# Blocks 0 and 1 of a masked graph kernel: first-layer result, e1 sums, table and first batches placed one slot sooner

## The chip, the cores and the metric

One NeuronCore of one Trainium2 chip runs the whole program. The metric is the device time in microseconds (us) of one execution; the median of three runs is compared.

## The reference, cut to what matters

`x` is 8192 by 128 in float32, `adj` 8192 by 8192 in int32, symmetric, with about 0.2% of entries 1 and the rest 0. Two graph layers follow each other, each with a residual and a normalization of the rows.

```python
o = (adj == 1) @ (x @ w1) + (adj == 2) @ (x @ w2) + (adj == 3) @ (x @ w3) + bias
x = layernorm(x + o)
h = x @ W.T + b
e = (h @ we1 + be1) + (h @ we2 + be2).T
e = where(e >= 0, e, 0.01 * e)
attention = softmax(where(adj > 0, e, -9e15), axis=1)
x = layernorm(x + attention @ h)
```

## The kernel before, in words

**Blocks, chunks and slots.** The 8192 rows are 8 blocks (S) of 1024, each block's columns 8 chunks of 1024. Every engine's program is written out by hand as one loop over slots `k`. In slots 0 to 63 slot k takes in chunk k: GpSimd (POOL) issues the load of 1 MB (`load`, L527 to L535; four homes, so load k waits until chunk k-4 is packed), VectorE (DVE) packs it into bits (`check_and_pack`, L586 to L617), ScalarE (ACT) converts it (`convert`, L1121), TensorE (PE) turns it (`turn`, L1348), and ACT copies it out of PSUM one slot later (`edges_of`, L1136). One slot later DVE makes the two halves of 0/1 masks of chunk k-1 (`edge_masks`, L630), and two slots later PE multiplies them in 32 matmuls, 16 a half (`layer0(k-2, h)`, L1333). `turn` is of blocks 0 to 3 alone; later blocks are turned by DMA.

**The tail of a block.** `tails(k)` (L360) gives for each slot the blocks S and their offset `off = k - 8(S+1)`. At off 1 ACT copies the block's sums (`y_of`, L1154) and PE multiplies them by w1 (`o_of(S, 0)`, L1355) into PSUM bank 3. At off 2 DVE adds x (`v_of(S, 0)`), PE makes `o_of(S, 1)` into the same bank between the two halves of layer0, having waited for `v_of(S, 0)`, and after packing DVE runs `v_of(S, 1)`, `statistics` (L670) and, at the slot's end, `rs_of` (L682), with ACT's square root `sd_of` (L1162) between them. At off 3 ACT writes the normalized rows x1 (`x1_of`, L1166), DVE forms the sums with two vectors (`e_sums`, L688: products at L693, sums at L697 and L700, constants at L704 and L707), between its two mask halves, and PE turns e1 (`e1_turn`, L1369) at the end of its slot. At off 4 ACT copies e1 out (`e1_turned`, L1182), makes exponentials (`b_d_of`) and the high half of the block's table (`high`, L1187); DVE makes the low half (`low`, L718) at off 4 in block 0 and off 5 in block 1; in later blocks its two parts come at off 5 and 6. SyncE (SP) stores x1 and then e1 (`tail`, L399), and reads e1 back as a row on all partitions (`row_of`, L416).

**Batches.** The second layer is 128 batches (`batch(m)`, L1374) of 32 matmuls, one group of 512 rows with one chunk of columns. A batch needs the table of its chunk, the group's e1 row, eight ACT passes over that row (`gates`, L1140), and four bit passes and two logical passes on DVE (`masks`, L639). 48 of them are spread over slots 13 to 68, the rest runs from slot 69 with one batch a slot. `EARLY` (L57) says which batches come behind which block, and `plan` (L72) puts block b's first one in slot `8(b+1) + START` with START 5. Batches 0 and 1 stand in slots 13 and 14; batches 2 to 7 in slots 21, 22, 23, 25, 26 and 27; from slot 29 every slot has one. Block b's first batch is `fresh` (L126): its gates come after `convert` on ACT, those of other batches before it, in the slot ahead. The very first batch is placed behind the turning (`first_of_all`, L131). The sums of batch segment q go to banks 4 and 5 for even q, 6 and 7 for odd q (`z_bank`, L249), and DVE takes them out a batch later (`collect`, L754). At the end of a slot in which a segment ends, DVE prepares its exponents (`exponents`, L732), for which the partial sum before must have been stored.

**Order on a queue.** Each engine takes its instructions strictly in the order written. What stands behind a waiting instruction waits too.

Of the kernel before, what the change touches and what calls it, by code (L numbers as in the profile page):

```python
# [31 lines left out]
NS = 8  # L32
# [22 lines left out]
START = 5  # L55

EARLY = {  # L57
# [14 lines left out]
def plan():  # L72

    segs, slots, seen = [], [], {}
    for b, part in EARLY.items():
        segs += part
        n = sum(len(c) for _, c in part)
        slots += [NCH * (b + 1) + START + (i * NCH // n if n >= 6 else i) for i in range(n)]
        for g, c in part:
            seen.setdefault(g, set()).update(c)  # L80
    for g in LATE:
        segs.append((g, [c for c in range(NS) if c not in seen.get(g, ())]))
    early = len(slots)
    slots += [max(K + START, slots[-1] + 1) + i for i in range(16 * NS - early)]
    return segs, slots
# [40 lines left out]
def fresh(m):  # L126

    return SLOTS[m] == NCH * (BATCH[m][1] // 2 + 1) + START

# [11 lines left out]
def build(nc, x, adj, w1, w2, w3, bias, W, b, we1, be1, we2, be2, out):  # L141
# [4 lines left out]
    with ExitStack() as ctx:  # L146
# [98 lines left out]
        def o_of_bank(S, h):  # L245

            return ps[:, 2, :].rearrange("p (t c) -> p t c", t=GT) if h and S >= PAIRS else o_bank

# [128 lines left out]
        def _(e):  # L377
# [20 lines left out]

            def tail(S):  # L399
                e.wait_ge(s_x1, S + 1)  # L400
                e.dma_start(block_rows(x1_dram, S), X1[:, :, :]).then_inc(s_x1st, 16)
                e.wait_ge(s_e1Tc, S + 1)
                e.dma_start(e1_dram[S], e1T[:, :]).then_inc(s_e1st, 16)

# [54 lines left out]
            for S in range(NS - 1):  # L459
                tail(S)  # L460
                row_of(q)
                next_rows(S)
                for n in range(len(EARLY[S])):
                    if n + 1 < len(EARLY[S]):
                        row_of(q + 1)
                    if q:
                        part_store(q - 1)
                    part_load(q)
                    q += 1
            for S in STAGED:  # L470
                table_load(S)
            row_of(LOWS)
            tail(NS - 1)
            row_of(LOWS + 1)
# [98 lines left out]
        def _(e):  # L573
# [114 lines left out]
            def e_sums(S, parts=(0, 1)):  # L688
                sl = slice(JC * S, JC * (S + 1))
                e.wait_ge(s_x1, S + 1)  # L690
                e.wait_ge(s_setc, 1)
                for n in parts:
                    e.tensor_tensor((yT8, xg[:, :, :])[n], X1[:, :, :],  # L693
                                    u_b[:, n, :].unsqueeze(1).broadcast_to([P, RB, D]), ALU.mult).then_inc(s_pe, 1)
                if 0 in parts:
                    e.wait_ge(s_pe, 2 * S + 1)
                    e.reduce_sum(e1c[:, sl], yT8, AX).then_inc(s_e1c, 1)  # L697
                if 1 in parts:
                    e.wait_ge(s_pe, 2 * S + 2)
                    e.reduce_sum(t2[:, sl], xg[:, :, :], AX).then_inc(s_er, 1)  # L700
                if 0 in parts:
                    e.wait_ge(s_setc, 2)
                    e.wait_ge(s_e1c, 2 * S + 1)
                    e.tensor_scalar(e1c[:, sl], e1c[:, sl], c_sum[:, :], None, ALU.add).then_inc(s_e1c, 1)  # L704
                if 1 in parts:
                    e.wait_ge(s_er, S + 1)
                    e.tensor_scalar(t2c[:, sl], t2[:, sl], T2MAX, -T2MAX, ALU.min, ALU.max).then_inc(s_t2c, 1)  # L707
# [228 lines left out]
            for k in range(NSLOT):  # L936
                for S, off in tails(k):
                    if off == 2 and S < NS - 1:
                        v_of(S, 0)
                for m in at(k):  # L940
                    if not first_of_all(m):
                        masks(m)
                        after(m)
# [4 lines left out]
                for S, off in tails(k):  # L948
                    if off == 2:
                        if S == NS - 1:  # L950
                            v_of(S, 0)
                        v_of(S, 1)
                if 1 <= k <= K:
                    edge_masks(k - 1, 0)
                for S, off in tails(k):
                    if off == 2:
                        statistics(S)
                    if off == 3 and S < NS - 1:
                        e_sums(S)
                    if off == 3 and S == NS - 1:  # L960
                        rs_of(S)
                    if off in (4, 6) and S == NS - 1:
                        e_sums(S, ((off - 4) // 2,))
# [10 lines left out]
                for S, off in tails(k):  # L974
                    if off == 0:
                        x_and_bias(S)
                    if off == 2 and S < NS - 1:
                        rs_of(S)
                    if (S, off) in ((0, 4), (1, 5)):
                        low(S)  # L980
# [129 lines left out]
        def _(e):  # L1110
# [136 lines left out]
            for k in range(NSLOT):  # L1247
                for S, off in tails(k):
                    if off == 3 and S < NS - 1:
                        x1_of(S)  # L1250
# [4 lines left out]
                for S, off in tails(k):  # L1255
                    if off == (4 if S < NS - 1 else 6):
                        e1_turned(S)
                    if off == (4 if S < NS - 1 else 7):
                        b_d_of(S)
# [3 lines left out]
                for S, off in tails(k):  # L1263
                    if off == 4 and not S:
                        high(S)
                if k < PAIRS * NCH:
                    convert(k)
                elif k < K:
                    turn_pairs(k)
                for S, off in tails(k):  # L1270
                    if off == 2:
                        sd_of(S)
                if k < NCH:
                    split_high(k)
                for S, off in tails(k):
                    if off == 1:
                        y_of(S)
                    if off == 4 and 0 < S < NS - 1:
                        high(S, (0,))
# [6 lines left out]
                for S, off in tails(k):  # L1286
                    if off == 4 and 0 < S < NS - 1:
                        high(S, (2,))
                    if off == 3 and S == NS - 1:
                        x1_of(S)  # L1290
# [41 lines left out]
        def _(e):  # L1332
# [22 lines left out]
            def o_of(S, h):  # L1355
                e.wait_ge(s_y, 2 * S + h + 1)
                if h:
                    if S < PAIRS:
                        e.wait_ge(s_v, 2 * S + 1)
# [14 lines left out]
            def batch(m):  # L1374
# [5 lines left out]
                if first:  # L1380
                    ge(e, s_ev, q - 1)
                    if q == 0:
                        e.wait_ge(s_setc, 1)
                e.wait_ge(s_pos, m + 1)
                both = UP[:, 4096 * (m % 2):4096 * (m % 2 + 1)], gate_bufs[GATE[m]]
# [54 lines left out]
            for k in range(NSLOT):  # L1440
                if 2 <= k < K + 2:
                    layer0(k - 2, 0)
                for S, off in tails(k):
                    if off == 4 and PAIRS <= S < NS - 1:
                        e1_turn(S)
                    if off == 2 and S < NS - 1:
                        o_of(S, 1)
# [12 lines left out]
                for S, off in tails(k):  # L1460
                    if off == 1:
                        o_of(S, 0)
                        if S == NS - 1:
                            o_of(S, 1)
                    if off == 3 and S < PAIRS or off == 5 and S == NS - 1:
                        e1_turn(S)
# [99 lines left out]
```

## Time and profile before

| | |
|---|---|
| three runs | 1488.92, 1488.93, 1489.4 us, median 1488.93 |
| profiled execution | 1488.94 us, of which 1487.3 us lie between first and last instruction |
| granted TensorE clock, mean | 0.987 |
| busy time | PE 1391.1 us, DVE 1120.1, ACT 922.0, POOL 64.3 |
| loads of adj | 64, of 1 MB each in the kernel's memory |

The share of a busy engine is an average over stages: one with loads and one slot after another, and one with batches alone. An idle stretch of PE counts only where nothing later absorbs it.

### The profile page before, as it was taken

What the parts mean: (1) busy time and instruction counts of PE and PEld (TensorE: products, weight loads), DVE (VectorE), ACT (ScalarE), POOL (GpSimd) and SP (SyncE); (2) the same over time, 40 slices, a digit from 0 to 9 for tenths busy, and PEclk for the clock granted to TensorE, in tenths of its full rate; (3) what the DMA queues carried; (4) which work ended last, traced back from release to release, by engine and by line L of the source; (5) the groups of instructions that cost most, each with busy time, mean ns of one, the idle gap of its engine ahead of it and who ended that gap; (6) DMA issues with size and microseconds to landing.
All of it is one profiled execution on the core that took longest, in us unless ns stands there. A gap on an engine that the chain in (4) does not pass through costs nothing.

```text
span 1487.3 us, 18911 instructions
## 1 busy us (share of the span) xinstructions
PE 1391.1 (94%) x6678; PEld 651.6 (44%) x6678; DVE 1120.1 (75%) x2568; ACT 922.0 (62%) x1521; POOL 64.3 (4%) x73
## 2 busy tenths in 40 slices
PE   0787898999999999999999999999999999999996
PEld 0333343444444444444444444444444444444443
DVE  2668777988988978978978957776666777776664
ACT  1333525466546436345345459887888989988873
POOL 1101010000000000000000000000000000000000
PEclk9999899999999999999999999999999999999998
DMA  9999999996989989997999521000000111110000
GB/s 124 148 117 117 117 112 127 120 121 83 92 112 118 95 88 110 103 126 84 116 112 111 99 99 43 22 29 29 29 29 29 50 29 36 50 29 22 22 0 16
DMA packets 104786, 115.86 MB, mean 78 GB/s; under 512 B 21424, under 2 KB 87792, under 8 KB 104688
## 3 DMA queue, kind: packets, MB, share of 16 engines
q0 software_dynamic: 66560, 67.11, 49.5%
q1 hardware_dynamic: 20720, 43.30, 8.7%
q10 hardware_dynamic: 17408, 4.20, 1.8%
q8 instruction: 55, 0.90, 0.2%
q14 instruction: 43, 0.35, 0.1%
HBM read 295.44 MB, written 16.29 MB: 210 GB/s over the span
## 4 chain that ended last, share of the span: by engine, by line
PE 78%; DMA 9%; DVE 7%; ACT 4%; issue 2%; another core or an unknown queue 0%; POOL 0%; ACTq 0%; DVEq 0%; SPq 0%; POOLq 0%
PE ps L1389 56%; PE ps L1342 20%; DMA tables<-adj 8%; ACT neg_masks L1149 2%; DVE edge_masks L627 1%; PE ps L1404 1%; DVE seen L594 1%; PE ps L1366 1%; DVE neg_masks L647 1%; DVE tables L725 1%; DVE tables L591 0%; ACT tables L1198 0%; DVE adj_in L591 0%; ACT x L1172 0%; PE ps L1352 0%
## 5 line engine op out<-in xcount | busy, mean ns | idle before, releaser
L1149 ACT ACTIVATE neg_masks<-e_row,cols 128x512 int8<-128x512 f32 x816 | 510.6, 709 | 183.7 <-PE ps L1389 134.3
L1389 PE MATMUL ps<-pos_masks,tables 128*128 128x512 fp8e4 x2048 | 610.4, 380 | 7.5 <-DVE pos_masks L649 7.4
L1389 PE MATMUL ps<-neg_masks,tables 128*128 128x512 fp8e4 x1632 | 486.5, 380 | 0.0
L1342 PE MATMUL ps<-edge_masks,tables 128*128 128x512 fp8e4 (+1 forms) x2048 | 463.3, 384 | 0.0
L1389 PEld LDWEIGHTS ps<-pos_masks,tables 128*128 128x128 f16 x2048 | 200.0, 98 | 247.8 <-issue 12.7
L1342 PEld LDWEIGHTS ps<-edge_masks,tables 128*128 128x128 f16 x2048 | 202.0, 99 | 238.9 <-issue 12.4
L1389 PEld LDWEIGHTS ps<-neg_masks,tables 128*128 128x128 f16 x1632 | 159.9, 98 | 193.6 <-issue 1.7
L627 DVE TENSOR_SCALAR pos_masks<-edges 128x512 uint16<-128x512 uint16 x512 | 114.4, 286 | 143.8 <-PE ps L1389 143.8
L647 DVE TENSOR_TENSOR neg_masks<-pos_masks,neg_masks 128x2048 uint16<-128x2048 uint16 x102 | 125.0, 1225 | 52.8 <-ACT neg_masks L1149 49.8
L627 DVE TENSOR_SCALAR edge_masks<-edges 128x512 uint16<-128x512 uint16 x512 | 127.1, 315 | 31.5 <-PE ps L1342 27.2
L1149 ACT ACTIVATE y_turned<-e_row,cols 128x512 int8<-128x512 f32 x208 | 130.2, 709 | 21.0 <-PE ps L1389 21.0
L649 DVE TENSOR_TENSOR pos_masks<-pos_masks,neg_masks 128x2048 uint16<-128x2048 uint16 x102 | 124.9, 1225 | 3.5
L1389 PE MATMUL ps<-y_turned,tables 128*128 128x512 fp8e4 x416 | 123.7, 379 | 0.0
L1124 ACT ACTIVATE packed_bf<-packed 128x1024 bf16<-128x1024 uint8 x32 | 36.3, 1135 | 126.3 <-DVE packed L604 126.2
L1352 PE MATMUL ps<-idb,packed_bf 128*128 128x128 bf16 x256 | 21.3, 231 | 68.1 <-ACT packed_bf L1124 68.0
L591 DVE SCALAR_TENSOR_TENSOR adj_in<-adj_in 128x1024 uint32<-128x1024 uint32 x42 | 51.2, 1218 | 35.6 <-DMA adj_in<-adj 35.6
L534 POOL DMA_DIRECT2D adj_in<-adj x42 | 41.5, 989 | 532.7 <-DVE packed L604 213.7
L1389 PEld LDWEIGHTS ps<-y_turned,tables 128*128 128x128 f16 x416 | 40.7, 98 | 49.1
L1203 ACT ACTIVATE a_c_rows<-a_c_rows 128x1024 f32<-128x1024 f32 x34 | 35.8, 1053 | 30.1 <-DVE a_c_rows L740 30.0
L1138 ACT ACTIVATE edges<-ps 128x1024 uint8<-128x1024 bf16 x32 | 32.5, 1015 | 32.9 <-PE ps L1352 32.9
L594 DVE TENSOR_TENSOR seen<-seen,adj_in 128x2048 uint16<-128x2048 uint16 x42 | 51.4, 1224 | 1.4
L1352 PEld LDWEIGHTS ps<-idb,packed_bf 128*128 128x128 bf16 x256 | 16.8, 103 | 79.5 <-ACT packed_bf L1124 47.6
(155 smaller groups left out, 851.5 us busy)
## 6 DMA issues: line engine op xcount, KB each, us to landing
adj_in<-adj POOLq DMA_DIRECT2D x42, 1024.0 KB, 16.4
tables<-adj POOLq DMA_DIRECT2D x14, 1024.0 KB, 35.0
e_row<-e_scratch SPq DMA_DIRECT2D x34, 256.0 KB, 4.0
edges<-adj POOLq DMA_DIRECT2D x8, 1024.0 KB, 14.1
part_scratch<-a_c_rows SPq DMA_DIRECT2D x18, 256.0 KB, 6.0
part_in<-part_scratch SPq DMA_DIRECT2D x18, 256.0 KB, 4.1
edges<-x SPq DMA_DIRECT2D x8, 512.0 KB, 6.8
x_scratch<-x SPq DMA_DIRECT2D x8, 512.0 KB, 7.3
```

The source lines that it names most:

```text
L534: e.dma_start(homes[HOME[k]].bitcast(F8C).rearrange("p (b c) -> p b c", b=RB), block_rows(adj, S)[:, :, c * CC:(c + 1) * CC]).then_inc(s_a ...
L591: e.scalar_tensor_tensor(a, bb, 4, a, ALU.logical_shift_right, ALU.bitwise_or).then_inc(s_p1, 1)
L594: e.tensor_tensor(seen[:, :], seen[:, :], a8.bitcast(U16), ALU.bitwise_or).then_inc(s_seen, 1)
L627: ins = e.tensor_scalar(dst[:, :, n, :], src, abs(by), MASK, shift, ALU.bitwise_and)
L647: e.tensor_tensor(n, u, n, ALU.bitwise_and).then_inc(s_neg, 1)
L649: e.tensor_tensor(u, u, n, ALU.bitwise_xor).then_inc(s_pos, 1)
L1124: e.activation(pkb[:, :].rearrange("p (j q) -> p j q", j=JC), pk[:, :].rearrange("p (q j) -> p j q", j=JC), ACT.Copy).then_inc(s_conv, 1)
L1149: ins = e.activation(place(gate_bufs[GATE[m]], j, g // 2).bitcast(I8), e1row[:, q % 2, :], ACT.Sign, bias=t2[:, JC * c + j:JC * c + j + 1])
L1203: e.activation(ac[:, :, :], ac[:, :, :], ACT.Exp).then_inc(s_exp, 1)
L1342: ins = e.matmul(ps[:, h, :], v_hl[:, i, JC * c + j, :], place(U0[:, 4096 * h:4096 * (h + 1)], j, S).bitcast(kind), start=c == 0 and j == ...
L1352: ins = e.transpose(psT[:, j * P:(j + 1) * P], pkb[:, j * P:(j + 1) * P], idb[:, :])
L1389: ins = e.matmul(z_bank(q, k), tab[:, c, 2 * k + i, j, :], place(mask, j, g // 2).bitcast(F8A), start=first and j == 0 and i == 0, stop=fi ...
```

## The change

A constant FIRST = 2 is added. For blocks 0 and 1:

- `plan` puts the block's first batch at `8(b+1) + 4`. Batches 0 and 1 move to slots 12 and 13; batches 2 to 7 to slots 20, 21, 22, 24, 25 and 26. All later batches stay, so slots 27 and 28 now have none.
- PE makes both `o_of` at off 1, back to back; the second goes to bank 5. It no longer waits for `v_of(S, 0)`; in block 1 it waits until segment 0 is collected. The first batch of segments 0 and 2 waits for both `v_of` of the block whose product stood in its bank.
- DVE runs `v_of` of both halves, `statistics` and `rs_of` ahead of the packing of off 2, in one piece, and `e_sums` between the mask halves of the same slot. `low` comes one slot sooner.
- ACT runs `sd_of` and `x1_of` at off 2 ahead of `convert`, and `e1_turned`, `b_d_of` and `high` at off 3.

For blocks 0 to 3 `e1_turn` now stands between the two halves of layer0: at off 3 in blocks 0 and 1, at off 4 in blocks 2 and 3 (before at the end of off 3). For blocks 0 to 6 SP stores e1 and issues the first row ahead of the store of x1. `e_sums` of every block does e1 to its end before it begins with the other product.

```diff
+FIRST = 2
+def first_slot(b):
+    return NCH * (b + 1) + (START - 1 if b < FIRST else START)
-        slots += [NCH * (b + 1) + START + (i * NCH // n if n >= 6 else i) for i in range(n)]
+        slots += [first_slot(b) + (i * NCH // n if n >= 6 else i) for i in range(n)]
...
-            return ps[:, 2, :].rearrange("p (t c) -> p t c", t=GT) if h and S >= PAIRS else o_bank
+            if h and (S < FIRST or S >= PAIRS):
+                return ps[:, 5 if S < FIRST else 2, :].rearrange("p (t c) -> p t c", t=GT)
+            return o_bank
...
-                tail(S)
+                e1_store(S)
                 row_of(q)
+                x1_store(S)
                 next_rows(S)
...
                     if off == 2 and S < NS - 1:
                         v_of(S, 0)
+                    if off == 2 and S < FIRST:
+                        v_of(S, 1)
+                        statistics(S)
+                        rs_of(S)
...
-                    if off == 2:
+                    if off == 2 and S >= FIRST:
                         statistics(S)
-                    if off == 3 and S < NS - 1:
+                    if off == (2 if S < FIRST else 3) and S < NS - 1:
                         e_sums(S)
...
-                    if (S, off) in ((0, 4), (1, 5)):
+                    if (S, off) in ((0, 3), (1, 4)):
                         low(S)
...
-                    if off == (4 if S < NS - 1 else 6):
+                    if off == (3 if S < FIRST else 4 if S < NS - 1 else 6):
                         e1_turned(S)
...
+                    if off == 2 and S < FIRST:
+                        sd_of(S)
+                        x1_of(S)
                 if k < PAIRS * NCH:
                     convert(k)
...
                 if h:
-                    if S < PAIRS:
+                    if S == 1:
+                        e.wait_ge(s_ev, 1)
+                    elif FIRST <= S < PAIRS:
                         e.wait_ge(s_v, 2 * S + 1)
...
+                    if q in (0, 2):
+                        e.wait_ge(s_v, 2 + q)
...
-                    if off == 4 and PAIRS <= S < NS - 1:
+                    if off == (3 if S < FIRST else 4) and S < NS - 1:
                         e1_turn(S)
-                    if off == 2 and S < NS - 1:
+                    if off == 2 and FIRST <= S < NS - 1:
                         o_of(S, 1)
...
                         o_of(S, 0)
-                        if S == NS - 1:
+                        if S < FIRST or S == NS - 1:
                             o_of(S, 1)
-                    if off == 3 and S < PAIRS or off == 5 and S == NS - 1:
+                    if off == 5 and S == NS - 1:
                         e1_turn(S)
```

## Rows read from the trace of the kernel before

**Rows 1.** The page, busy time of each engine and its share of the span:

```profile
PE 1391.1 (94%) x6678; PEld 651.6 (44%) x6678; DVE 1120.1 (75%) x2568; ACT 922.0 (62%) x1521; POOL 64.3 (4%) x73
```

**Rows 2.** Windows: start:end, width, busy PE, PEld, DVE, ACT, POOL, PEclk, DMA share, GB/s:

```profile
144.00:156.00 12.00, 6.97 (x26) 2.92 (x27) 10.46 (x20) 7.96 (x20) 1.23 (x2) 0.72 1.11 139
```

**Rows 3.** Waits of PE from 266 us: total, times, longest:

```profile
PE ps L1389 <- DVE pos_masks L649: 4.7, 5, 1.6
```

**Rows 4.** Timeline of PE, block 0: start, duration, instruction, idle before and releaser:

```profile
115.69 0.62 PE L1352 MATMUL ps<-idb,packed_bf 128*128 128x128 bf16 x8 [2.35 <-ACT packed_bf L1124]
...
116.14 7.07 PE L1342 MATMUL ps<-edge_masks,tables 128*128 128x512 fp8e4 x32
...
126.06 1.16 PE L1366 MATMUL ps<-w_sb,y_turned 128*128 128x128 f32 x8
...
149.65 0.38 PE L1372 MATMUL ps<-idf,cols 128*8 128x128 f32 x1 [3.68 <-DVE cols L704]
...
172.35 1.03 PE L1352 MATMUL ps<-idb,packed_bf 128*128 128x128 bf16 x8 [5.47 <-ACT packed_bf L1124]
...
174.37 1.01 PE L1389 MATMUL ps<-pos_masks,tables 128*128 128x512 fp8e4 x2 [0.99 <-DVE pos_masks L649]
...
183.57 7.07 PE L1342 MATMUL ps<-edge_masks,tables 128*128 128x512 fp8e4 x32
```

**Rows 5.** Timeline of PE, block 1 and the batches behind it:

```profile
221.10 1.11 PE L1366 MATMUL ps<-w_sb,y_turned 128*128 128x128 f32 x8
...
237.64 0.62 PE L1352 MATMUL ps<-idb,packed_bf 128*128 128x128 bf16 x8 [0.28 <-ACT packed_bf L1124]
...
242.16 0.38 PE L1372 MATMUL ps<-idf,cols 128*8 128x128 f32 x1 [3.90 <-DVE cols L704]
...
242.33 9.53 PE L1342 MATMUL ps<-edge_masks,tables 128*128 128x512 fp8e4 x32
...
260.96 0.59 PE L1389 MATMUL ps<-pos_masks,tables 128*128 128x512 fp8e4 x2 [1.74 <-DVE pos_masks L649]
...
283.93 7.07 PE L1342 MATMUL ps<-edge_masks,tables 128*128 128x512 fp8e4 x32
```

**Rows 6.** Timeline of PE, block 2 and the first batch of slot 29:

```profile
320.08 1.11 PE L1366 MATMUL ps<-w_sb,y_turned 128*128 128x128 f32 x8
...
357.45 0.61 PE L1352 MATMUL ps<-idb,packed_bf 128*128 128x128 bf16 x8
...
366.62 0.59 PE L1389 MATMUL ps<-pos_masks,tables 128*128 128x512 fp8e4 x2 [1.65 <-DVE pos_masks L649]
```

**Rows 7.** Timeline of DVE, block 1:

```profile
228.74 1.63 DVE L673 BATCH_NORM_STATS2 stats<-x_rows 128x6 f32<-128x128 f32 x8
...
232.30 1.22 DVE L591 SCALAR_TENSOR_TENSOR tables<-tables 128x1024 uint32<-128x1024 uint32 x1
...
237.36 1.22 DVE L693 TENSOR_TENSOR y_turned<-x,u_rows 128x1024 f32<-128x1024 f32 x1
...
242.09 0.89 DVE L627 TENSOR_SCALAR edge_masks<-edges 128x512 uint16<-128x512 uint16 x4
...
258.33 1.23 DVE L647 TENSOR_TENSOR neg_masks<-pos_masks,neg_masks 128x2048 uint16<-128x2048 uint16 x1 [4.65 <-ACT neg_masks L1149]
...
268.68 2.17 DVE L725 SCALAR_TENSOR_TENSOR tables<-x,cols,tables 128x127 f16<-128x127 f32 x8
```

**Rows 8.** Timeline of ACT, block 1:

```profile
248.08 2.43 ACT L1198 ACTIVATE tables<-x,cols 128x127 f16<-128x127 f32 x8
...
253.21 5.01 ACT L1149 ACTIVATE neg_masks<-e_row,cols 128x512 int8<-128x512 f32 x8 [2.59 <-issue]
```

**Rows 9.** DMA issues at 235.6, 154.4 and 353.1: count, KB, us to landing:

```profile
x_scratch<-x SPq DMA_DIRECT2D x1, 512.0 KB, 7.6
...
e_row<-e_scratch SPq DMA_DIRECT2D x1, 256.0 KB, 6.0
...
e_row<-e_scratch SPq DMA_DIRECT2D x1, 256.0 KB, 3.8
```

More of the change, by code:

```diff
@@ L126, in fresh @@
 def fresh(m):
-    return SLOTS[m] == NCH * (BATCH[m][1] // 2 + 1) + START
+    return SLOTS[m] == first_slot(BATCH[m][1] // 2)
 def first_of_all(m):
@@ L397, in _, with e1_store, x1_store @@
                 x_piece(v)
-            def tail(S):
+            def e1_store(S):
+                e.wait_ge(s_e1Tc, S + 1)
+                e.dma_start(e1_dram[S], e1T[:, :]).then_inc(s_e1st, 16)
+            def x1_store(S):
                 e.wait_ge(s_x1, S + 1)
                 e.dma_start(block_rows(x1_dram, S), X1[:, :, :]).then_inc(s_x1st, 16)
-                e.wait_ge(s_e1Tc, S + 1)
-                e.dma_start(e1_dram[S], e1T[:, :]).then_inc(s_e1st, 16)
             def next_rows(S):
@@ L472, in _ @@
             row_of(LOWS)
-            tail(NS - 1)
+            x1_store(NS - 1)
+            e1_store(NS - 1)
             row_of(LOWS + 1)
@@ L694, in e_sums @@
                                     u_b[:, n, :].unsqueeze(1).broadcast_to([P, RB, D]), ALU.mult).then_inc(s_pe, 1)
-                if 0 in parts:
-                    e.wait_ge(s_pe, 2 * S + 1)
-                    e.reduce_sum(e1c[:, sl], yT8, AX).then_inc(s_e1c, 1)
+                    if n == 0:
+                        e.wait_ge(s_pe, 2 * S + 1)
+                        e.reduce_sum(e1c[:, sl], yT8, AX).then_inc(s_e1c, 1)
+                        e.wait_ge(s_setc, 2)
+                        e.wait_ge(s_e1c, 2 * S + 1)
+                        e.tensor_scalar(e1c[:, sl], e1c[:, sl], c_sum[:, :], None, ALU.add).then_inc(s_e1c, 1)
                 if 1 in parts:
@@ L700, in e_sums @@
                     e.reduce_sum(t2[:, sl], xg[:, :, :], AX).then_inc(s_er, 1)
[L701 to L705, printed above, removed]
                     e.wait_ge(s_er, S + 1)
@@ L951, in _ @@
                             v_of(S, 0)
-                        v_of(S, 1)
+                        if S >= FIRST:
+                            v_of(S, 1)
                 if 1 <= k <= K:
@@ L1248, in _ @@
                 for S, off in tails(k):
-                    if off == 3 and S < NS - 1:
+                    if off == 3 and FIRST <= S < NS - 1:
                         x1_of(S)
@@ L1255, in _ @@
                 for S, off in tails(k):
-                    if off == (4 if S < NS - 1 else 6):
+                    if off == (3 if S < FIRST else 4 if S < NS - 1 else 6):
                         e1_turned(S)
-                    if off == (4 if S < NS - 1 else 7):
+                    if off == (3 if S < FIRST else 4 if S < NS - 1 else 7):
                         b_d_of(S)
@@ L1263, in _ @@
                 for S, off in tails(k):
-                    if off == 4 and not S:
+                    if off == 3 and not S:
                         high(S)
+                    if off == 2 and S < FIRST:
+                        sd_of(S)
+                        x1_of(S)
                 if k < PAIRS * NCH:
@@ L1270, in _ @@
                 for S, off in tails(k):
-                    if off == 2:
+                    if off == 2 and S >= FIRST:
                         sd_of(S)
@@ L1277, in _ @@
                         y_of(S)
-                    if off == 4 and 0 < S < NS - 1:
+                    if off == (3 if S < FIRST else 4) and 0 < S < NS - 1:
                         high(S, (0,))
@@ L1286, in _ @@
                 for S, off in tails(k):
-                    if off == 4 and 0 < S < NS - 1:
+                    if off == (3 if S < FIRST else 4) and 0 < S < NS - 1:
                         high(S, (2,))
@@ L1443, in _ @@
                 for S, off in tails(k):
-                    if off == 4 and PAIRS <= S < NS - 1:
+                    if off == (3 if S < FIRST else 4) and S < NS - 1:
                         e1_turn(S)
-                    if off == 2 and S < NS - 1:
+                    if off == 2 and FIRST <= S < NS - 1:
                         o_of(S, 1)
```

## The prediction

> **What bounds the kernel now.** I read the page first: PE is busy 94% of the span [rows 1], so time can only come from idle stretches of PE or from its clock. The waits of PE say where they are: from 266 us to the end the longest-named wait, for masks, adds up to 4.7 us in five pieces [rows 3]. So behind 266 us PE itself is the bound, and whatever lead or lag it has there goes into the end. Ahead of that I read PE's timeline. A slot with one chunk costs PE 6.9 us for 32 matmuls (the printed 7.07 includes the last one's tail) and 0.45 us for the turn: 7.35 us together; a batch costs 6.9. Up to slot 9 the loads set the pace, with gaps of 2.35 us before each turn at the full clock [rows 4]. In block 0's tail PE waits 3.68 us for e1's sums, 5.47 for the converted chunk behind two sets of gates, and 0.99 for masks [rows 4]; in block 1's tail 0.28, 3.90 and 1.74 [rows 5]. Behind the long gaps the clock falls: the 12 us round the gap of 3.68 show a granted clock of 0.72 on average [rows 2], part of it at 1.2 of 2.4 GHz. A chunk's matmuls then take 9.53 instead of 7.07 [rows 5], and batch 0 lasts from 174.37 to 183.57, 9.2 instead of 6.9 [rows 4].
>
> The work of PE stays the same, so I lay the changed order out by hand with the durations of these rows and compare at points where both kernels have done the same work.
>
> **Block 0.** PE's first product starts at 126.06 [rows 4]; the second now follows 0.95 later. DVE adds the second half at 128.2, and the way from statistics to the last operation of `rs_of` is 232.30 - 228.74 = 3.6 us less 0.4 for a mask half that stood in it and covered part of the square root: 3.2 [rows 7]. Adding 0.65 for the second addition (estimate, half of a 1.22 pass over 1024 elements), packing of chunk 10 starts at 132.0, and turning follows 5.3 later (232.30 to 237.64 [rows 5, 7]), at 137.4. PE has been done since 134.9: a new gap of 2.5. `e_sums` takes 242.09 - 237.36 = 4.7 [rows 7], plus 0.5 (estimate) since its new order makes each step wait for the one before: 5.2. It stands between the mask halves, so layer0's second half waits 1.5. Then `high`, twice 2.43 [rows 8], stands ahead of `convert`: a gap of 3.3, turn at 149.8. But e1 is turned at 141.25, not 149.65 [rows 4], 8.4 sooner. From there the order is the old one (copy, store, row, gates, edges, gates, convert), 22.7 us to the turn at 172.35 [rows 4]: now 164.0, with a gap of 6.9. The low table, twice 2.17 [rows 7], and packing are done before; they cost nothing, and had 1 us to spare. The masks are ready at 163.1, so the wait of 0.99 goes, and batch 0 runs from 165.0 to 174.85 at the falling clock. That is 8.7 sooner than 183.57, with one chunk less behind it: 8.7 - 7.35 = 1.4 us ahead, and 0.2 more at a later turn, so **1.6 ahead** when block 1's product starts (219.5 against 221.10 [rows 5]). The slow clock after the gap of 3.68 goes because there is nothing behind the new gaps but waiting. Loads: the packing of chunks 10 and 11 is 2 to 3 us later, so loads 14 and 15 are issued later; three others stand ahead of them on POOL's queue, which I take as cover. If it went, packing would wait those 3 us, once.
>
> **Block 1.** The same steps from 219.5: DVE adds at 221.75, packs chunk 18 from 225.65, turn at 231.05; PE was done at 228.4, gap 2.6. e1 is turned at 234.95 against 242.16 [rows 5], 7.2 sooner; the second half waits 1.4 for its masks; turning of chunk 19 is at 241.95, gap 1.8. layer0 of chunk 18 ends at 249.3. From e1's turning to batch 2 the rows show 260.96 - 242.16 = 18.8 [rows 5], of which the row lands just ahead of 253.21 [rows 8] and gates, masks and releases take 7.75. So batch 2 starts at 253.75: a gap of 4.45. The gaps add up to 10.2, where they were 5.9, since there is one chunk less (7.35) to lie beside a chain that has become only 5.6 shorter (34.25 against 39.86). The clock falls once in both. Batch 2 ends at 263.0, then come turn, chunk 19 and batch 3 without a gap, and chunk 20 starts at 277.5, against 283.93 - 7.35 = 276.6. **0.9 behind**, so 2.5 of loss after 1.6 of lead. The wait of the first product on bank 5 is over long before, as is that of batch 2 for `v_of`.
>
> **Block 2.** Its first product starts after four slots of 7.35 and three batches: 277.5 + 29.4 + 20.7 = 327.7. Batch 7 has gone from slot 27 to 26, so slots 27 and 28 are without one while DVE does block 2's sums. DVE from 328.9: addition 0.6, masks of batch 7 3.35 (four bit passes, then two of 1.23 [rows 7]), packing 4.05, addition 0.6, mask half 0.8, statistics 2.55, mask half 0.8, `rs_of` 0.4, exponents 0.7: 342.75. Packing to 346.8, a wait to 347.35 for PE, mask half 0.8, sums 5.2, mask half 0.8: packing of chunk 28 starts at 354.15 and its turn is at 359.45, against 357.45 [rows 6]. Half of `high` (2.4) and 7.75 later batch 8 starts at 369.5, against 366.62 [rows 6]: **2.9 behind**, PE idle for 1.1 and 2.7 where it was idle for 1.65. In the slots behind, both orders are the same, and PE has no slack to win it back.
>
> **The sum**: -1.6, +2.5, +2.0 = +2.9 us. On the profiled execution, 1487.3 of span and 1488.94 in all, that makes 1491.8; the median of the runs is the same to 0.01.
>
> **Two places where a price is not shown.** What the row costs when it is issued ahead of x1's store: rows landed after 6.0 and, in block 2, 3.8 [rows 9]. I take 6.0, since the adj stream is as dense in blocks 0 and 1 as it was; 3.8 is the other end. The block's second row now stands behind the store, which alone took 7.6 [rows 9]; between 0 and 7.6 later. I take no delay beyond the 2 us that block 0 has to spare.
>
> The clock could also fall sooner in block 1, on the gaps of 2.6, 1.4 and 1.8 together; then chunk 18 is the slow one, which the wait for batch 2 absorbs, and the sum would be +2.2. The Trainium skill (TensorE: Matmul & The Clock Gate, "The HAM clock gate") says the throttled state is the default and activity releases it; by that reading spread-out gaps count as well, and the rows, where 2.35 alone did no harm, do not decide it.
>
> **Rivals.** A, faster: the first row, now with no store ahead of or beside it, lands in 3.8. Then gates come 2.2 sooner in both blocks, in block 0 only 1.9 of it is usable, and in block 1 the gap before batch 2 is 2.25, below the 2.35 at which the clock held [rows 4]; batch 2 takes 6.9, masks of batch 3 become the limit, and the point of 277.5 is reached 3.2 sooner. With block 2's extra 2.0 hidden this gives 0.9 - 3.2 - 1.9 = -4.2, 1484.7; without, -2.2. It decides if batch 2 starts before 251.6. Against it: 6.0 [rows 9]. Chance 0.18.
>
> B, no difference: block 2's slots have room that my sum of DVE lacks (2 us in 26): +0.9, 1489.8. Chance 0.22.
>
> C, slower still: the second row of block 0 comes 2.4 after it is wanted, at 160.3 (issued at 146.7, 7.6 of store, 6.0 of row), and everything behind moves: +5.3, 1494.2; with one more slow stretch (2.5) 1496.7. Chance 0.20. The Trainium skill (DMA: Bandwidth & Descriptors, "Queues, rings and completion order") says that each engine consumes one queue's descriptors in ring order, and takes turns between queues. That rule gives C's order on SP's queue; no row here shows a row behind a store.
>
> **How the numbers follow.** The forecast itself has 0.40; its error of some 2 us either way puts 0.24 of it above 0.2% (3.0 us, about what a measurement of this kernel can tell from no change) and 0.16 within. Slower 0.24 + 0.20 = 0.44, within 0.16 + 0.22 = 0.38, faster 0.18. The range goes from 1486.0, which takes in half of A, to 1496.5, almost all of C.
>
> **What would show it.** Right: e1's turnings near 141 and 235; turns of chunks 12 and 19 near 164 and 242; batch 2 near 254 with a gap over 4 us and a slow stretch; block 1's product at 219.5; batch 8 at 369.5 with PE idle over 2 us before it; behind that a constant distance. Wrong: a row that lands in under 5 us, gates waiting for the second row, packing that waits for a load after chunk 12, or a distance that shrinks behind 370 us.

## The result and the profile after

| | before | changed |
|---|---|---|
| median of 7 runs each, taken side by side | 1488.19 us | 1493.63 us |
| lowest to highest | 1486.45 to 1489.4 | 1490.81 to 1496.99 |
| span of the profiled execution | 1487.3 | 1491.9 |

The ratio is 1.004, with a 95% interval of 1.0031 to 1.0049: slower by 5.4 us as a difference of medians, 5.9 by the ratio. The changed kernel's runs also lie further apart, 6.2 us against 3.0. Of all executions below, two of the kernel before and one of e2 took 1870 to 7680 us; the ratios leave these three out.

The page of the changed kernel, its span and its busy time, answers to [rows 1]:

```profile
span 1491.9 us, 18912 instructions
...
PE 1396.7 (94%) x6678; PEld 654.3 (44%) x6678; DVE 1121.3 (75%) x2568; ACT 922.7 (62%) x1521; POOL 68.4 (5%) x73
```

PE is busy 5.6 us longer, though its program has the same 6678 matmuls. With the same instructions that points to matmuls at a lower clock. But 3.2 us of the 5.6 lie before slot 9's turn (71.1 us busy against 68.0), where both kernels have the same program and the loads set the pace; behind it PE is busy 2.5 us longer and idle 3.6 us longer.

PE's timeline in block 0, against [rows 4]. Columns: start, duration, instruction, idle before and releaser. The first two rows are slot 7, where both kernels have the same program:

```profile
104.31 0.85 PE L1374 MATMUL ps<-idb,packed_bf 128*128 128x128 bf16 x8 [2.35 <-ACT packed_bf L1143]
...
104.96 8.56 PE L1364 MATMUL ps<-edge_masks,tables 128*128 128x512 fp8e4 x32
...
124.05 0.62 PE L1374 MATMUL ps<-idb,packed_bf 128*128 128x128 bf16 x8 [2.36 <-ACT packed_bf L1143]
...
124.53 3.36 PE L1390 MATMUL ps<-w_sb,y_turned 128*128 128x128 f32 x16
...
137.21 0.62 PE L1374 MATMUL ps<-idb,packed_bf 128*128 128x128 bf16 x8 [2.07 <-ACT packed_bf L1143]
...
141.12 0.27 PE L1396 MATMUL ps<-idf,cols 128*8 128x128 f32 x1
...
149.65 1.03 PE L1374 MATMUL ps<-idb,packed_bf 128*128 128x128 bf16 x8 [3.07 <-ACT packed_bf L1143]
...
164.01 1.03 PE L1374 MATMUL ps<-idb,packed_bf 128*128 128x128 bf16 x8 [5.54 <-ACT packed_bf L1143]
...
174.00 7.07 PE L1364 MATMUL ps<-edge_masks,tables 128*128 128x512 fp8e4 x32
```

The turns and e1's turning (L1396, the small transpose) stand where the prediction laid them: 137.21, 141.12, 149.65, 164.01. But this execution reached slot 9 1.5 us sooner than the one before (124.05 against 125.58), and lost that on two products at the lower clock (3.36 for the 16 matmuls; the same pair took 2.00 in block 1). So the agreement to 0.1 us is partly luck. Chunk 11's matmuls start at 174.00.

Block 1, against [rows 5]:

```profile
218.88 2.00 PE L1390 MATMUL ps<-w_sb,y_turned 128*128 128x128 f32 x16
...
230.19 0.62 PE L1374 MATMUL ps<-idb,packed_bf 128*128 128x128 bf16 x8 [2.40 <-ACT packed_bf L1143]
...
230.65 5.30 PE L1364 MATMUL ps<-edge_masks,tables 128*128 128x512 fp8e4 x16
...
235.79 0.27 PE L1396 MATMUL ps<-idf,cols 128*8 128x128 f32 x1
...
241.53 0.62 PE L1374 MATMUL ps<-idb,packed_bf 128*128 128x128 bf16 x8 [1.60 <-ACT packed_bf L1143]
...
254.40 1.01 PE L1415 MATMUL ps<-pos_masks,tables 128*128 128x512 fp8e4 x2 [5.35 <-DVE pos_masks L665]
...
277.85 7.07 PE L1364 MATMUL ps<-edge_masks,tables 128*128 128x512 fp8e4 x32
```

e1 is turned 6.4 us sooner than before, 2.2 of it because block 1's first product came that much sooner, and batch 2 waits 5.35 us for its masks where it waited 1.74. Half a chunk of matmuls ahead of e1's turning took 5.30 us, not the 3.62 that it takes at the full clock.

Block 2 and slot 29, against [rows 6]:

```profile
328.29 1.11 PE L1390 MATMUL ps<-w_sb,y_turned 128*128 128x128 f32 x8
...
360.41 0.62 PE L1374 MATMUL ps<-idb,packed_bf 128*128 128x128 bf16 x8 [1.48 <-ACT packed_bf L1143]
...
370.41 0.68 PE L1415 MATMUL ps<-pos_masks,tables 128*128 128x512 fp8e4 x2 [2.48 <-DVE pos_masks L665]
...
379.00 0.61 PE L1374 MATMUL ps<-idb,packed_bf 128*128 128x128 bf16 x8
```

A gap of 1.48 before the turn of chunk 28 and 2.48 before batch 8 stand where there was one of 1.65, and from batch 8 to the turn of slot 29 it takes 8.59 us where it took 7.5.

The waits of PE from 266 us on, against [rows 3]:

```profile
PE ps L1415 <- DVE pos_masks L665: 5.9, 5, 2.5
...
PE ps L1374 <- ACT packed_bf L1143: 1.5, 1, 1.5
```

**Everything is decided by the turn of slot 29.** From that turn to the end of the span the kernel before takes 1487.3 - 374.14 = 1113.2 us and the changed one 1491.9 - 379.00 = 1112.9; the eleven kernels below take 1112.6 to 1113.3. Ahead of slot 9's turn all have the same program, and that turn comes at 124.1 to 126.1 us in the profiled executions. So three stretches between tell the story: A from the turn of slot 9 to block 1's first product, B from there to the turn of slot 28 (by then every kernel has done batches 0 to 7), C to the turn of slot 29. They are read from the profiled executions:

| kernel | A | B | C | median us | ratio to before, interval |
|---|---|---|---|---|---|
| before | 95.5 | 136.4 | 16.7 | 1488.2 | |
| changed | 94.8 | 141.5 | 18.6 | 1493.6 | 1.004 (1.0031 to 1.0049) |
| e1, small edits alone | 92.9 | 135.6 | 17.4 | 1487.4 | 1.0002 (0.9993 to 1.0011) |
| e2, block 0 alone | 95.5 | 135.5 | 17.4 | 1489.0 | 1.0008 (0.9999 to 1.0018) |
| e3, batch 7 back | 95.4 | 138.7 | 17.5 | 1491.6 | 1.0024 (1.0015 to 1.0033) |
| e4, all batches back | 92.7 | 134.3 | 18.5 | 1485.7 | 0.9983 (0.9974 to 0.9993) |
| e5, e1 turned between halves | 94.1 | 136.4 | 16.7 | 1487.9 | 1.0 (0.9991 to 1.0009) |
| e6, batches 2 to 7 back | 95.1 | 134.3 | 17.4 | 1487.4 | 0.9993 (0.9984 to 1.0002) |
| e7, e4 and block 2's turning back | 92.4 | 134.3 | 18.4 | 1486.7 | 0.9992 (0.9983 to 1.0001) |
| e8, changed, waits filled | 94.7 | 139.2 | 17.5 | 1490.0 | 1.0012 (1.0003 to 1.0021) |
| e9, e7, waits filled | 93.4 | 134.3 | 17.3 | 1485.4 | 0.9984 (0.9975 to 0.9993) |
| e10, before, waits filled | 93.2 | 137.6 | 16.7 | 1487.1 | 0.9993 (0.9984 to 1.0002) |
| e11, batches 0 and 1 back | 94.6 | 141.4 | 18.6 | 1493.5 | 1.0035 (1.0022 to 1.0049) |

The medians of the kernel before, measured beside the others, were 1487.8 to 1488.3, so the ratios compare better than the medians. e11 has 5 runs, the changed kernel 7, the others 11.

One profiled execution is one draw of where the clock falls. In A the same program took 92.4, 92.7 and 94.6 (e7, e4 and e11), in C 17.4 and 18.5 (e6 and e4). B repeats to 0.1 where the program is the same (134.3 for e4 and e6, 135.6 and 135.5 for e1 and e2, 141.5 and 141.4 for changed and e11). The profiled executions of e1 and e7 were the fastest of their eleven (1486.07 and 1483.75 us), that of e8 the slowest (1491.36).

### The profile page after: what moved, and what is told of

It reads as the page before. It is cut to its first block, busy times and chain, and to the rows that moved or that the text cites. A ratio compares the mean times of both kernels' runs of the same rounds, so it can differ in the third digit from the quotient of the medians.

```text
span 1491.9 us, 18912 instructions
## 1 busy us (share of the span) xinstructions
PE 1396.7 (94%) x6678; PEld 654.3 (44%) x6678; DVE 1121.3 (75%) x2568; ACT 922.7 (62%) x1521; POOL 68.4 (5%) x73
## 4 chain that ended last, share of the span: by engine, by line
PE 80%; DMA 9%; DVE 6%; ACT 4%; issue 1%; ACTq 0%; POOL 0%; DVEq 0%; SPq 0%; POOLq 0%
PE ps L1415 57%; PE ps L1364 20%; DMA adj_in<-adj 7%; ACT neg_masks L1168 3%; PE ps L1390 1%; PE ps L1430 1%; DVE seen L610 1%; DMA e_row<-e_scratch 1%; PE ps L1374 1%; DVE neg_masks L663 1%; DMA e_scratch<-e_turned 1%; DVE adj_in L607 0%; ACT packed_bf L1143 0%; DVE pos_masks L665 0%; ACT tables L1217 0%
## 5 line engine op out<-in xcount | busy, mean ns | idle before, releaser
L1415 PEld LDWEIGHTS ps<-pos_masks,tables 128*128 128x128 f16 x2048 | 200.5, 98 | 252.6 <-issue 18.4
```

Of the source, the lines that this page charges most:

```text
L1415: ins = e.matmul(z_bank(q, k), tab[:, c, 2 * k + i, j, :], place(mask, j, g // 2).bitcast(F8A), start=first and j == 0 and i == 0, stop=fi ...
```

## The experiments

**e1, the small edits alone.**

```diff
-FIRST = 2
+FIRST = 0
```

(with the wait of block 1's second product, `low` and `high` as in the kernel before)

> Only what the change does to every block: e1's turning between the halves of layer0, x1's store behind the first row, e1 summed to its end first. Blocks 0 and 1 keep their old slots. Theory (the loss comes from moved batches that leave PE without work while the chain of sums runs): the chain to batch 0 is as long as before, batch 2 starts near 261 as before but with a longer gap before it, so a slow stretch may fall on the batch: +0 to +2.4 us in block 1, +1.4 in block 2 because the row comes after the high table. Together 0 to +4, most likely +2. Rival (these small edits are the whole loss): +5.4, the same as the changed kernel.

Measured 1.0002. The small edits are not the loss. Two rows of its PE timeline in block 0 and the one of batch 8:

```profile
149.34 0.27 PE L1394 MATMUL ps<-idf,cols 128*8 128x128 f32 x1
...
151.19 3.63 PE L1364 MATMUL ps<-edge_masks,tables 128*128 128x512 fp8e4 x16 [1.58 <-DVE edge_masks L643]
...
364.01 0.59 PE L1413 MATMUL ps<-pos_masks,tables 128*128 128x512 fp8e4 x2 [2.40 <-DVE pos_masks L665]
```

In block 0 e1 is turned as late as before (149.34), but half a chunk of matmuls lies beside the wait, which has shrunk from 3.68 to 1.58. In block 2 the small edits cost: batch 8 waits 2.40 instead of 1.65. That is not the row's doing, as e7 shows below. The forecast of +2 was too high.

**e2, block 0 alone.**

```diff
-FIRST = 2
+FIRST = 1
```

(with the wait of block 1's second product and its `low` as in the kernel before)

> FIRST = 1: block 0 alone is moved, block 1 keeps its slots (21 to 27). Theory: block 0 by itself brings a lead of about 1.6 us, so this kernel is 1 to 2 us faster than the kernel with FIRST = 0, some +0.4 against before, and PE shows no long gap before batch 8. Rival (block 0 is where the time is lost): 3 us or more slower than the kernel with FIRST = 0.

Measured 1.0008: no gain over e1, by the medians 1.5 us slower than it, with overlapping intervals. Block 0's move brought no lead here; A is 95.5, as long as before, where e1 has 92.9. Neither was it where the changed kernel lost 5 us.

**e3, batch 7 back in slot 27.**

```diff
+    slots[7] = 27
     early = len(slots)
```

> The changed kernel with batch 7 back in slot 27, batches 2 to 6 left a slot sooner. Theory: the gaps of 1.48 before the turn of chunk 28 and 2.48 before batch 8, and the slow stretch behind, go for the most part: 3 to 4 us faster than the changed kernel, some +1.5 against before. Rival (everything is lost in block 1 before batch 2): no faster than the changed kernel, +5.

Measured 1.0024, 2.0 us less than the changed kernel by the medians: half of what was expected. Slots 28 and 29:

```profile
359.27 0.62 PE L1375 MATMUL ps<-idb,packed_bf 128*128 128x128 bf16 x8 [0.52 <-ACT packed_bf L1144]
...
369.27 0.59 PE L1416 MATMUL ps<-pos_masks,tables 128*128 128x512 fp8e4 x2 [2.48 <-DVE pos_masks L666]
...
376.79 0.62 PE L1375 MATMUL ps<-idb,packed_bf 128*128 128x128 bf16 x8 [0.45 <-ACT packed_bf L1144]
```

The gap of 1.48 is 0.52 now, and batch 8 runs at the full clock (7.5 us to the next turn), but its own wait of 2.48 has stayed: it comes from the small edits, as in e1. What is left, 3.6 us against before, must lie with the other seven batches, the tail or the small edits.

**e4, the tails moved, the batches not.**

```diff
-    return NCH * (b + 1) + (START - 1 if b < FIRST else START)
+    return NCH * (b + 1) + START
```

> The changed kernel with all batches in their old slots (13, 14, 21 to 23, 25 to 27), so that only x1, e1, the exponents and the table come a slot sooner. Theory: the chain of e1 is still 6 to 8 us sooner, and now a chunk of layer0 more lies beside it; the gap before batch 2 goes from 5.35 to under 1 and slots 26 to 28 are as before: -4 to -6 us against before, 1483 to 1485. Rival (the tail packed into one slot is itself the loss, by the gaps it makes before the turns of chunks 10, 11, 18 and 19): +2 or more.

Measured 0.9983 (0.9974 to 0.9993), 1485.7 us: faster than both kernels, by less than expected. PE in slots 13, 19 and 21:

```profile
170.28 0.62 PE L1374 MATMUL ps<-idb,packed_bf 128*128 128x128 bf16 x8 [2.17 <-ACT packed_bf L1143]
...
172.59 1.01 PE L1415 MATMUL ps<-pos_masks,tables 128*128 128x512 fp8e4 x2 [1.69 <-DVE pos_masks L665]
...
235.28 0.27 PE L1396 MATMUL ps<-idf,cols 128*8 128x128 f32 x1
...
241.02 0.62 PE L1374 MATMUL ps<-idb,packed_bf 128*128 128x128 bf16 x8 [1.59 <-ACT packed_bf L1143]
...
257.37 0.59 PE L1415 MATMUL ps<-pos_masks,tables 128*128 128x512 fp8e4 x2 [1.48 <-DVE pos_masks L665]
```

With the old slots a chunk of layer0 runs where the changed kernel waits: batch 2 waits 1.48, not 5.35, and B is 134.3, 2.1 less than before. The tail packed into one slot is thus not the loss; by e1, which has the small edits alone, it is a gain of some 2 us (1.0002 to 0.9983, intervals that touch). The loss is the batches moved after it. The difference between e4 and the changed kernel, 7.9 us in the medians, is one line of the plan.

**e5, only e1's turning between the halves in blocks 0 and 1, on the kernel before.**

```diff
-                    if off == 4 and PAIRS <= S < NS - 1:
+                    if off == 4 and (S < 2 or PAIRS <= S < NS - 1):
                         e1_turn(S)
-                    if off == 3 and S < PAIRS or off == 5 and S == NS - 1:
+                    if off == 3 and 2 <= S < PAIRS or off == 5 and S == NS - 1:
```

> The kernel before with one edit: in blocks 0 and 1 e1 is turned between the two halves of layer0 of slot off 4 instead of at the end of off 3, so half a chunk of matmuls lies beside the wait for e1's sums. Theory from the runs so far (the kernel with FIRST = 0 reached block 1's first product 2.6 us sooner after its slot 9 and lost time only before batch 8): block 0 gains 2 to 3 us, block 1 about nothing, block 2 is as before: 2 to 3 us faster than before, 1485 to 1486. Rival (the gain there came from the sums' order or from the store of x1 behind the row): no difference, within 0.5 us of before.

Measured 1.0. The theory of 2 to 3 us fell. e1's short A came from its fastest execution, so it was probably a lucky draw of the clock in large part. What PE no longer waits before e1's turning it waits before batch 2 (4.94 in its profile).

**e6, batches 2 to 7 back, 0 and 1 moved; e11, the other way round.**

e6:

```diff
-    return NCH * (b + 1) + (START - 1 if b < FIRST else START)
+    return NCH * (b + 1) + (START - 1 if b < 1 else START)
```

e11:

```diff
-    return NCH * (b + 1) + (START - 1 if b < FIRST else START)
+    return NCH * (b + 1) + (START - 1 if b == 1 else START)
```

> Both tails a slot sooner as in the changed kernel, batches 0 and 1 in slots 12 and 13 as in the changed kernel, batches 2 to 7 in their old slots. Theory: moving batches 0 and 1 takes a chunk of layer0 away from beside the chain of row, gates and conversion, 2 to 3 us slower than the kernel with all old slots (1485.7): about 1488.2. Rival (only batches 2 to 7 cost anything): within 0.5 us of 1485.7.

> The changed kernel with batches 0 and 1 back in slots 13 and 14; batches 2 to 7 stay in slots 20 to 26. Theory (block 0's batches cost about 2.4 us and block 1's about 5, and they add): 1.5 to 2.5 us faster than the changed kernel, +3.5 to +4 against before. Rival (the two are one cost, paid once): as slow as the changed kernel.

e6 measured 0.9993, e11 1.0035. Against e4 (1485.7), moving batches 0 and 1 costs 1.7 us, moving 2 to 7 costs 7.7; the two kernels ran with different runs of the kernel before, and the intervals of 1.3 us and more leave the 1.7 uncertain. e11 is as slow as the changed kernel, and B is the same to 0.1 (141.4 and 141.5). So nearly the whole loss is block 1's batches, and the part ascribed to batches 0 and 1 was too high.

**e7, e4 with e1's turning of blocks 2 and 3 at the old place.**

```diff
-                    if off == (3 if S < FIRST else 4) and S < NS - 1:
+                    if off == (3 if S < FIRST else 4) and (S < FIRST or PAIRS <= S < NS - 1):
                         e1_turn(S)
-                    if off == 5 and S == NS - 1:
+                    if off == 3 and FIRST <= S < PAIRS or off == 5 and S == NS - 1:
```

> The kernel with all old slots, and e1's turning of blocks 2 and 3 put back to the end of off 3. Theory: block 2's row comes sooner, the gap before batch 8 falls from 2.39 back to 1.65 or less and the slow stretch behind it goes: 0.7 to 2 us faster than the kernel with old slots, 1484 to 1485. Rival (the row is not what batch 8 waits for): no difference.

Measured 0.9992 (1486.7). No gain over e4; the wait before batch 8 was 2.24 instead of 2.39. Where e4 ran faster by the medians, the intervals overlap. The rival named ahead of the run holds: batch 8 does not wait for the row. ACT in block 2, first of the kernel before, then of e7, shows what it waits for:

```profile
355.42 1.14 ACT L1124 ACTIVATE packed_bf<-packed 128x1024 bf16<-128x1024 uint8 x1 [1.81 <-DVE packed L604]
...
358.89 4.99 ACT L1149 ACTIVATE neg_masks<-e_row,cols 128x512 int8<-128x512 f32 x8
...
349.65 1.15 ACT L1143 ACTIVATE packed_bf<-packed 128x1024 bf16<-128x1024 uint8 x1 [2.38 <-DVE packed L620]
...
353.14 4.99 ACT L1168 ACTIVATE neg_masks<-e_row,cols 128x512 int8<-128x512 f32 x8
```

In both, the gates for batch 8 start without idle time right behind `high`, which stands behind `convert`, and `convert` waits for DVE's packing. Measured from slot 28's turn (357.45 and 351.11), the gates start 1.44 later in the kernel before and 2.03 later in e7. The 0.6 between them is what the new order of `e_sums` costs DVE ahead of that packing: from its first product to the next mask half it takes 5.30 us (338.71 to 344.01) instead of 4.72 (345.06 to 349.78). The wait before batch 8 grew by the same 0.6, from 1.65 to 2.24. In block 1 it is otherwise: there the changed kernel's row was issued at 240.60 and landed 6.0 later, and the gates started at 246.66 after an idle 2.75.

**e8, the changed kernel with its waits filled.**

```diff
+            def fill(s, value, n):
+                e.wait_ge(s, value)
+                for _ in range(n):
+                    e.matmul(ps[:, 3, 0:P], idb[:, :], idb[:, :], start=True, stop=True)
...
+                if k in (10, 18):
+                    fill(s_v, 2 * (k // 8), 24)
+                if k in (20, 29):
+                    fill(s_e1Tc, 2 + k // 29, 56 if k == 20 else 30)
+                if k == 28:
+                    fill(s_e1Tc, 3, 16)
```

> The changed kernel with small matmuls (128 columns, results used by nobody) in the waits: 24 behind layer0 in slots 10 and 18, 56 before batch 2, 16 in slot 28 and 30 before batch 8. It adds work and takes no wait away. Theory of the clock (about 1.7 us before e1's turning, 1.8 to 2.4 on batch 2 and 1 on batch 8 are matmuls at 1.2 GHz): 2.5 to 4.5 us faster than the changed kernel, and a narrower spread of its runs. Rival (the gaps alone are the loss, the clock is absorbed by later waits): no difference or up to 1 us slower.

`fill` waits until the bank it writes is free and then runs n small matmuls, whose results nobody uses. Measured 1.0012 (1490.0): the added matmuls made the changed kernel 3.6 us faster by the medians, and its runs lie 3.2 us apart instead of 6.2. Windows of the changed kernel (start:end, width, busy PE, PEld, DVE, ACT, POOL, granted clock, DMA share, GB/s):

```profile
228.00:240.00 12.00, 9.49 (x41) 3.94 (x41) 11.27 (x21) 4.36 (x7) 0.99 (x1) 0.86 1.13 108
...
252.00:264.00 12.00, 9.60 (x42) 4.21 (x43) 11.79 (x26) 10.10 (x21) 0.98 (x1) 0.74 1.06 113
...
366.00:378.00 12.00, 9.52 (x37) 3.86 (x36) 10.02 (x18) 11.88 (x23) 0.98 (x1) 0.86 0.75 88
```

The same windows of e8:

```profile
228.00:240.00 12.00, 9.02 (x66) 4.91 (x65) 11.27 (x21) 5.36 (x10) 0.99 (x1) 1.00 1.12 108
...
252.00:264.00 12.00, 11.10 (x74) 5.63 (x71) 11.79 (x29) 11.29 (x23) 0.98 (x1) 1.00 1.09 119
...
366.00:378.00 12.00, 10.74 (x79) 5.78 (x77) 11.28 (x23) 11.29 (x22) 0.98 (x1) 1.00 0.70 82
```

and two rows of its PE timeline:

```profile
235.11 0.27 PE L1396 MATMUL ps<-idf,cols 128*8 128x128 f32 x1
...
253.62 0.59 PE L1415 MATMUL ps<-pos_masks,tables 128*128 128x512 fp8e4 x2 [0.44 <-DVE pos_masks L665]
```

The granted clock is 1.00 where it was 0.86, 0.74 and 0.86, of two levels, 1.2 and 2.4 GHz. e1 is turned 3.91 us after the turn at 231.20, where the changed kernel took 5.60 from 230.19; batch 2 starts 18.5 later. B is 2.3 us shorter than in the changed kernel and C 1.1.

**e9 and e10, the same filling in the faster order and in the kernel before.** e9 adds it to e7 (24 small matmuls in slots 10 and 18, 36 in slot 11, 20 in slot 13, 24 in slot 29); e10 to the kernel before (44 ahead of e1's turning in blocks 0 and 1, 60 in slot 13, 16 in slot 29).

```diff
+                if k in (10, 18):
+                    fill(s_v, 2 * (k // 8), 24)
+                if k in (11, 13):
+                    fill(s_e1Tc, 1, 36 if k == 11 else 20)
+                if k == 29:
+                    fill(s_e1Tc, 3, 24)
```

> Both tails a slot sooner, all batches in their old slots, e1's turning of blocks 2 and 3 as before, and small matmuls (128 columns, results used by nobody) in the waits of slots 10, 11, 13, 18 and 29. Theory (what is left of the loss of the clock in this order is the slow stretch ahead of e1's turning in blocks 0 and 1 and behind batch 0 and batch 8): 2 to 4 us faster than the same order without the small matmuls (1486.7), 1483 to 1485, and 4 to 5 us faster than before. Rival (the clock is absorbed): no difference from 1486.7.

> The kernel before with small matmuls in its own waits: 44 ahead of e1's turning in blocks 0 and 1, 60 ahead of the turn of slot 13, 16 ahead of batch 8. Theory: batch 0 takes 6.9 instead of 9.2 us, the slow chunk behind block 1's turning is absorbed by the wait for batch 2: 2 to 3 us faster than before, so the small matmuls bring the changed kernel more (3.6) than they bring this one. Rival (the clock costs both orders the same): 3.5 us or more faster.

e9 measured 0.9984 (0.9975 to 0.9993), 1485.4: 1.3 us less than e7 by the medians, but the intervals overlap, and it is not clear of e4 either. The turns of slots 10 and 18 and e1's turnings in e9:

```profile
136.61 0.62 PE L1374 MATMUL ps<-idb,packed_bf 128*128 128x128 bf16 x8 [1.07 <-ACT packed_bf L1143]
...
140.52 0.27 PE L1396 MATMUL ps<-idf,cols 128*8 128x128 f32 x1
...
229.44 0.62 PE L1374 MATMUL ps<-idb,packed_bf 128*128 128x128 bf16 x8 [1.06 <-ACT packed_bf L1143]
...
233.35 0.27 PE L1396 MATMUL ps<-idf,cols 128*8 128x128 f32 x1
```

Both distances are 3.91, so the chain never meets the slow clock there; in A the time comes back as waiting before slot 13. e10 measured 0.9993 (1487.1), 1.0 to 1.3 us less than before where 2 to 3 were expected, with an interval that takes in no difference. Two of its rows:

```profile
172.11 1.03 PE L1352 MATMUL ps<-idb,packed_bf 128*128 128x128 bf16 x8 [3.23 <-ACT packed_bf L1124]
...
258.06 1.01 PE L1389 MATMUL ps<-pos_masks,tables 128*128 128x512 fp8e4 x2 [4.06 <-DVE pos_masks L649]
```

The turn of slot 13 is still slow (1.03, the full clock gives 0.62) and so is batch 2, behind a wait of 4.06 that the earlier saving has turned into. So filling gave the changed order some 3.6 us back and the old order about one, if anything. What the clock costs in all is not shown, since e10 left two slow stretches, and e8 left those of slots 9 and 12.

## Why the prediction came out as it did

It was right in sign and in place, and the time lies in its range; the size was half of what was measured (+2.9 against +5.4 to 5.9). Summed over A, B and C the profiled executions differ by 6.3 us; slot 9's turn came 1.5 sooner in the changed one, which leaves 4.6 in the spans.

- **Block 0, laid out as 1.6 of lead.** The steps were right one by one: start of packing 132.0 (131.85 measured), gaps of 2.5, 1.5 and 3.3 (2.07, 1.56, 3.07), e1's turning, the turn at 164.0. The gap before it was 5.54, not 6.9, because chunk 10 ran slow, which that wait absorbed. But the lead was not there: A is 0.7 shorter in the profiled execution, which had slow products at its start, and e2 and e6 show 0.0 and 0.4. The failed step is the start: the laid-out order began at 126.06 with the full clock, and I had written that gaps of 2.35 do no harm. From slot 9's turn to the start of packing I had 6.4 us; measured were 7.8, since the two products took 3.36 instead of 2.0. In e11 they took 3.61 and A was 94.6; in e4 and e7, with the same program there, 2.05 and A was 92.7 and 92.4. A second error hid part of this: batch 0 was laid out at 9.85 us (165.0 to 174.85), though its row gives 9.2 and it took 9.16 (164.84 to 174.00). By the row, the lead laid out would have been 2.2, not 1.6.
- **Block 1, +2.5.** From block 1's product to the start of chunk 20 I laid out 58.0; measured were 277.85 - 218.88 = 59.0, against 276.6 - 221.10 = 55.5 before: +3.5. The 1.0 that was missing is the half chunk of 5.30 us ahead of e1's turning, directly on the chain, less what ran a little faster. "Then chunk 18 is the slow one, which the wait absorbs" put the slow stretch in the wrong place: it was the chunk before, ahead of e1's turning, and nothing absorbs that. Batch 2 ran slow besides, as laid out.
- **Block 2, +2.0.** From chunk 20 to batch 8: 92.56 against 90.0 before, +2.5, near the forecast, with gaps of 1.48 and 2.48 for 1.1 and 2.7. The layout had batch 8 behind `high` and `convert`, and the longer `e_sums` ahead of them, and that is what e7's rows show. On top came 1.07 from batch 8 to the turn of slot 29, at the fallen clock; that step was not in the sum. e3 (2.0 by the medians) and e8 (C 1.1 shorter) bear out both parts.
- **The clock as a term.** The sum for block 1 counted one slow stretch in each order and let them cancel. Filling gave back 3.6 in e8 and about 1.2 in e10. The difference, 2.4, is about what the forecast lacked, but the intervals reach 1.3 us to either side, so this fit proves little. The rows show 1.0 in block 1 and 1.07 behind batch 8.
- **Rival A** (the first row in 3.8) did not come: 6.3 and 6.0 in the rows below, as taken. **Rival B**, that block 2 costs nothing, is refuted by the 92.56 against 90.0, and e3 bears that out. **Rival C** was near its edge. DMA landings of the changed kernel: first row of block 0, first row of block 1, second row of block 0:

```profile
e_row<-e_scratch SPq DMA_DIRECT2D x1, 256.0 KB, 6.3
...
e_row<-e_scratch SPq DMA_DIRECT2D x1, 256.0 KB, 6.0
...
e_row<-e_scratch SPq DMA_DIRECT2D x1, 256.0 KB, 11.0
```

and ACT's gates for batches 0 and 1:

```profile
152.12 5.01 ACT L1168 ACTIVATE neg_masks<-e_row,cols 128x512 int8<-128x512 f32 x8 [2.52 <-DMA e_row<-e_scratch]
...
157.03 1.00 ACT L1157 ACTIVATE edges<-ps 128x1024 uint8<-128x1024 bf16 x1
...
157.94 4.99 ACT L1168 ACTIVATE neg_masks<-e_row,cols 128x512 int8<-128x512 f32 x8
```

The second row was issued at 146.74 behind x1's store and landed 11.0 later, at 157.74; the gates that need it could start at 157.94. It came 0.2 us in time. x1's store, issued at 146.22, landed 9.6 later. In the kernel before, block 0's second row, behind the first row alone, landed 7.6 after its issue. The Trainium skill (DMA: Bandwidth & Descriptors, "Queues, rings and completion order") has one queue's descriptors consumed in ring order on each engine; the 11.0 against 7.6 without a store ahead agree with it.

Open is how the 7.7 us of e11 against e4 split exactly: B gives 7.1, of which gaps before batch 2 (5.21 against 1.48) are 3.7, a slow batch 2 1.7 (8.77 us to the next turn against 7.06), and the gap in slot 28 the rest. A version with batches 3 to 7 moved and batch 2 left was not tried. Nor was the old order of `e_sums` tried in e4, where it should give back about 0.6 us before batch 8 (an estimate from e7's rows).

## What to carry to other kernels

When a chain of small steps becomes shorter, the work that lies beside it should stay there; moving the next consumer forward by a whole slot takes more work away from beside the chain (a chunk, 7.35 us) than the chain gives (4.3 us here: from block 1's first product to batch 2 it takes 35.5 us instead of 39.9), and the bound engine waits. Shorten the chain and leave the plan alone: e4 gained 2.5 us where the change lost 5.9. Count slow stretches of TensorE as a term of the sum, by where each falls: here one cost up to 1.7 us ahead of e1's turning, on the chain, and one nothing in chunk 10 (8.00 us), ahead of a wait of 5.54.

## What the runs showed of the hardware

The clock fell behind short gaps as well, and not always. Between the turn of slot 10 or 18 and e1's turning all kernels with a moved tail run the same 16 matmuls of layer0: it is 3.91 us at the full clock and 5.5 to 5.6 when it has fallen. Behind a gap of 2.40 or 2.41 in slot 18 it was 5.6 in the changed kernel, e4, e7 and e11, and 3.91 in e3 and e6. In slot 10 it was 5.5 to 5.6 behind gaps of 2.33 to 2.41 in six kernels, and 3.91 behind 2.07 in the changed one. Behind gaps of 1.05 to 1.07, with small matmuls in front, it was 3.91 in all four cases of e8 and e9. Slot 7 of the changed kernel, 104.96 to 113.5, is slow behind a gap of 2.35, which [rows 4] alone had made look harmless. The Trainium skill (TensorE: Matmul & The Clock Gate, "The HAM clock gate") says that the number of matmuls that run slow at a kernel's start varies from run to run. No run here shows a start by itself, but the stretch in slot 18 varied in the same way: 5.60 in the changed kernel and 3.91 in e3, behind equal gaps. The spread of 6.2 us in the changed kernel's runs and of 3.2 with filled waits fits, though two sets of runs do not show it. Matmuls that compute nothing made a program on the engine that bounds it 3.6 us faster, as e8's forecast had it.
